# Start of a transformer block on one core: the order of the first loads and weight conversions, and identity matmuls ahead of the first rows

## The chip, the cores and the metric

The kernel runs on one core of a Trainium2 chip. The metric is the device time of one launch in microseconds. The runs shown of the kernel before gave 1534.84, 1535.05 and 1535.28 us, with a median of 1535.05 us.

## The reference

The input x is (2, 2048, 256) in fp32: 4096 rows (tokens) of 256 features. Cut to what matters, the reference computes

```
x = x + 0.5 * ffn(layernorm(x))
x = x + attention(layernorm(x))          # 16 heads of 16 features, softmax over 2048 keys
x = x + 0.5 * ffn(layernorm(x))

def ffn(x):                              # each weight is +1 or -1, from a boolean
    h = concatenate([x, -x], axis=-1)    # 512 features
    h = relu(s0 * (h @ where(k0, 1, -1))) * 2      # k0 (512, 1024)
    h = relu(s1 * (h @ where(k1, 1, -1))) * 2      # k1 (1024, 1024)
    return s2 * (h @ where(k2, 1, -1))             # k2 (1024, 256)
```

Only the start of the first ffn, on the first 512 rows, is touched by this change.

## The kernel before, in words

**Tiling.** The 4096 rows are cut into 8 blocks of 512 rows; a block is 4 tiles of 128 rows (`tpb = 4`). Block u goes through these steps, which a planner (`layers`, from line 146, and the list `side`, line 193) writes into one list `work`. Every engine then walks this list in order and issues its own share of each step.

- `norm`: VectorE takes the mean and variance of each row (`bn_stats`, `bn_aggr`) and forms 1/sqrt with a bit trick and three Newton rounds (`dve_norm`, line 947). The factor 64 times 2 times the sign of s0 (`scal[:, 12:13]`) is multiplied in there.
- `xn`: VectorE subtracts the mean and multiplies (`dve_xn`, line 992), four instructions, one for each tile.
- Turning features to partitions: for later blocks a DMA transpose does it. For block 0 alone TensorE does it (`turn_x`): for each of two feature halves m, four transposes of 128x128 against the identity `ident` into one PSUM bank. ScalarE then writes the fp16 rounded part of the bank to `xt[:, 0, m]`, and VectorE the fp16 rest to `xt[:, 1, m]`.
- `l1`: eight steps m, one for each 128 of the 1024 hidden features, four matmuls each (rounded part and rest, two halves of 128 features each). Since the second half of the concatenated input is -x, `w0` is the difference of two halves of k0 (`dve_w0`, line 600). ScalarE writes the rounded part `h0_hi` of each bank (L840), VectorE the rest `h0_lo` (L911).
- `l2`: eight steps of sixteen matmuls with `w1`: the eight rounded parts k = 0 to 7 first, then the eight rests. The first step waits for each `h0_hi[k]` and for each `w1[:, k]` as it comes to them.
- `l3` with `w2`, and for later steps the projections and the attention.

**Weights.** k0, k1 and k2 come as bytes. `w1` is made from k1 as fp16 in eight instructions of 128x1024: the four even k by ScalarE (`act_w1`, line 614), the four odd k by VectorE (`dve_w1`, line 608), all of them between `turn_x` and `l1` in the list. Two instructions of VectorE make `w0` columns 0 to 511 ahead of the turning and two make columns 512 to 1023 behind it. GpSimd makes the identity (L561, L564), then ten small instructions on the factors s0, s1, s2 (`pool_scalars`, line 580), then `w2` (L575) and scaled projection weights (L578).

**Loads.** They are issued ahead of all else, from two queues. ScalarE issues the three factors (4 bytes each, broadcast to 128 partitions) and k0 in two loads of 256 KB (`act_loads`, line 536). SyncE issues the four tiles of the first block (128 KB each), k1 in one load of 1 MB, block 1 (512 KB), k2, the projection weights and biases and block 2 (`sp_loads`, line 543).

**Order.** All engines are strictly in order on their lists. PSUM banks are handed out in a ring of seven in this part of the kernel; `l1` uses each at most once more, far behind its readers. For block 0 the list begins

```
side = norm_turn(0, 0) + [Step("w0", 0, 0)] + turns("turn_x", 0) + [Step("w0", 0, 1), Step("w1")]
side += [Step("l1", 0, m) for m in range(kh)]
```

TensorE's first wait is that all four tiles of `xn` are done (line 652). `norm` of block 1 stands in the list behind the second step of `l2` of block 0.

Of the kernel before, what the change touches and what calls it, by code (L numbers as in the profile page):

```python
# [13 lines left out]
ACT = mybir.ActivationFunctionType  # L14
ALU = mybir.AluOpType
AX = mybir.AxisListType

P = 128
# [5 lines left out]
class Step:  # L24
# [30 lines left out]
FILLS = {  # L55
    "turn_x": (4, (1, 1), (0, 2)),
    "l1": (4, (1, 1), (0, 2)),
# [30 lines left out]
def build(nc, x, wq, bq, wk, bk, wv, bv, wo_t, bo, k0, k1, k2, s0, s1, s2, out):  # L88
# [103 lines left out]

    side = norm_turn(0, 0) + [Step("w0", 0, 0)] + turns("turn_x", 0) + [Step("w0", 0, 1), Step("w1")]
    side += [Step("l1", 0, m) for m in range(kh)]
    for u in range(2 * blocks):
# [198 lines left out]
    with ExitStack() as ctx:  # L394
# [66 lines left out]
        def internal(name, shape, dt):  # L461
# [15 lines left out]
        k0_in = [sem(f"k0_in{k}") for k in range(kd)]  # L477
        scal_in, k1_in, k2_in, weights_in = (sem(n) for n in ("scal_in", "k1_in", "k2_in", "weights_in"))
        piece_out = [sem(f"piece_out{n}") for n in range(2 * kd)]
# [5 lines left out]
            sem(n) for n in ("consts", "scal_done", "table_seed", "table_ready"))  # L485
        w0_done, w1_act, w1_dve, w2_done, qk_scaled = (
            sem(n) for n in ("w0_done", "w1_act", "w1_dve", "w2_done", "qk_scaled"))

# [11 lines left out]
        CONSTS = 6  # L500
        IDENT = 3
        SCALARS = 10
        WEIGHTS_IN = 16 * 10
# [27 lines left out]
        def load_x(u):  # L531
            i = block_of(u)
            ts = slice(i * tpb, (i + 1) * tpb)
            sp.dma_start(x_sb[:, u % RING], (x_tiles if u < blocks else x1_tiles)[:, ts, :]).then_inc(x_in[u % RING], 16)

        def act_loads():
            for n, s in enumerate((s0, s1, s2)):
                act.dma_start(scal[:, n:n + 1], s.broadcast_to((P, 1))).then_inc(scal_in, 16)
            for k in range(kd):
                act.dma_start(k0_raw[:, k::kd, :], k0.rearrange("(h k p) n -> p k h n", p=P, k=kd)[:, k]  # L540
                              ).then_inc(k0_in[k], 16)

        def sp_loads():
            for t in range(tpb):
                sp.dma_start(x_sb[:, 0, t, :], x_tiles[:, t, :]).then_inc(x0_in[t], 16)
            sp.dma_start(k1_raw, k1.rearrange("(k p) n -> p k n", p=P)).then_inc(k1_in, 16)
            load_x(1)
            sp.dma_start(k2_raw, k2.rearrange("(k p) n -> p k n", p=P)).then_inc(k2_in, 16)
            for dst, src in ((wq_sb, wq), (wk_sb, wk), (wv_sb, wv), (wo_sb, wo_t)):
                sp.dma_start(dst[:], src.rearrange("(k p) n -> p k n", p=P)).then_inc(weights_in, 16)  # L550
            for dst, src in ((bq_sb, bq), (bk_sb, bk)):
                for k in range(kd):
                    sp.dma_start(dst[:, k:k + 1], src[k * hpt:(k + 1) * hpt].rearrange("h a e -> (h e) a")
                                 ).then_inc(weights_in, 16)
            sp.dma_start(bv_sb[:], bv.rearrange("h a e -> a (h e)").broadcast_to((P, dim))).then_inc(weights_in, 16)
            sp.dma_start(bo_sb[:], bo.rearrange("(a n) -> a n", a=1).broadcast_to((P, dim))).then_inc(weights_in, 16)
            for u in range(2, RING - 1):
                load_x(u)

        def pool_constants():  # L560
            pool.memset(ident[:], 0.0).then_inc(consts, 1)  # L561
            pool.memset(head_ones[:], 1.0).then_inc(consts, 1)
            pool.wait_ge(consts, 2)
            pool.affine_select(out=ident[:], in_=ident[:], compare_op=ALU.not_equal, fill=1.0, base=0,  # L564
                               pattern=[[-1, P]], channel_multiplier=1).then_inc(consts, 1)
            ho = head_ones[:].rearrange("p (h e) -> p h e", e=hd // 4)
            pool.affine_select(out=ho, in_=ho, compare_op=ALU.is_ge, fill=0.0, base=0,
                               pattern=[[-hd, hpt], [0, hd // 4]], channel_multiplier=1).then_inc(consts, 1)
            pool.wait_ge(consts, 4)
            pool.affine_select(out=ho, in_=ho, compare_op=ALU.is_ge, fill=0.0, base=hd - 1,  # L570
                               pattern=[[hd, hpt], [0, hd // 4]], channel_multiplier=-1).then_inc(consts, 1)
            pool.memset(v_sb[:, :, :, hd:va], 1.0).then_inc(consts, 1)
            pool_scalars()
            pool.wait_ge(k2_in, 16)
            pool.tensor_scalar(w2[:], k2_raw, 2.0, -1.0, ALU.mult, ALU.add).then_inc(w2_done, 1)  # L575
            pool.wait_ge(weights_in, WEIGHTS_IN)
            for w in (wq_sb, wk_sb, bq_sb, bk_sb):
                pool.tensor_scalar(w[:], w[:], QK_SCALE, 0.0, ALU.mult, ALU.add).then_inc(qk_scaled, 1)  # L578
# [21 lines left out]
        def dve_w0(m):  # L600

            cols = slice(m * hidden // 2, (m + 1) * hidden // 2)
            for k in range(kd):
                dve.wait_ge(k0_in[k], 16)
                dve.tensor_tensor(w0[:, k, cols], k0_raw[:, k, cols], k0_raw[:, kd + k, cols], ALU.subtract
                                  ).then_inc(w0_done, 1)

        def dve_w1():
            dve.wait_ge(k1_in, 16)
            for k in range(1, kh, 2):  # L610
                dve.tensor_scalar(w1[:, k, :], k1_raw[:, k, :], scal[:, 13:14], scal[:, 14:15], ALU.mult, ALU.add
                                  ).then_inc(w1_dve, 1)

        def act_w1():
            act.wait_ge(k1_in, 16)
            act.wait_ge(scal_done, SCALARS)
            for k in range(0, kh, 2):
                act.activation(w1[:, k, :], k1_raw[:, k, :], ACT.Identity, scale=scal[:, 13:14], bias=scal[:, 14:15]
                               ).then_inc(w1_act, 1)

        def pe_steps(steps):
            for s in steps:
# [12 lines left out]
                elif s.kind in FILLS and s.lo < s.hi:  # L637
                    pe_fill(s)

        def pe_fill(s):  # L640
            u, m, bank = s.u, s.m, s.bank
# [7 lines left out]
            for j in range(s.lo, s.hi):  # L649
                if s.kind == "turn_x":  # L650
                    if j == 0 and m == 0:
                        pe.wait_ge(ln_x, tpb)
                        pe.wait_ge(consts, IDENT)
                    mm = pe.transpose(psum[:, bank, j * P:(j + 1) * P], xn[:, 0, j, m * P:(m + 1) * P], ident[:])  # L654
                elif s.kind == "l1":
# [3 lines left out]
                    if u == 0 and m == 0 and half == 0:  # L659
                        wait_hi(pe, find["turn_x", u, k])  # L660
                        pe.wait_ge(w0_done, k + 1)
                    if u == 0 and m == kh // 2 and j < kd:
                        pe.wait_ge(w0_done, kd + k + 1)
                    if u == 0 and m == 0 and half == 1:
# [3 lines left out]
                elif s.kind == "l2":  # L668
                    half, k = divmod(j, kh)
                    if m == 0 and half == 0:  # L670
                        wait_hi(pe, find["l1", u, k])
                        if u == 0 and k % 2 == 0:
                            pe.wait_ge(w1_act, k // 2 + 1)
                        if u == 0 and k % 2 == 1:
                            pe.wait_ge(w1_dve, k // 2 + 1)
                    if m == 0 and half == 1:
# [148 lines left out]
        def act_steps(steps):  # L825
            for s in steps:
# [3 lines left out]
                elif s.kind == "w1":  # L830
                    act_w1()
                elif not s.on_act or s.kind not in FILLS or not s.last():
                    continue
                elif s.kind == "turn_x":
                    act.wait_ge(mm_done, s.mm)
                    act.activation(xt[:, 0, m, :], psum[:, bank, :], ACT.Copy).then_inc(act_done, 1)  # L836
                elif s.kind in ("l1", "l2"):
# [34 lines left out]
        def dve_steps(steps):  # L872
            for s in steps:
# [15 lines left out]
                elif s.kind == "w0":  # L889
                    dve_w0(m)  # L890
                elif s.kind == "w1":
                    dve_w1()
                elif s.kind not in FILLS or not s.last():
                    continue
                elif s.kind == "turn_x":
                    if s.on_act:
                        dve.wait_ge(act_done, s.act)
                    else:
                        dve.wait_ge(mm_done, s.mm)
                        dve.tensor_copy(xt[:, 0, m, :], psum[:, bank, :]).then_inc(dve_done, 1)  # L900
                        dve.wait_ge(dve_done, s.hi_dve)
                    dve.tensor_tensor(xt[:, 1, m, :], psum[:, bank, :], xt[:, 0, m, :], ALU.subtract).then_inc(dve_done, 1)
                elif s.kind in ("l1", "l2"):
# [43 lines left out]
        def dve_norm(s):  # L947
# [26 lines left out]
            for k in range(3):  # L974
                at_k = base + 2 * tpb + 4 + 3 * k
                dve.wait_ge(ln, at_k)
                dve.tensor_tensor(square_y, y, y, ALU.mult).then_inc(ln, 1)
                if k == 2 and n == 0:
                    dve.wait_ge(scal_done, SCALARS)
                if k == 2:  # L980

                    dve.tensor_scalar(root[:, 5, :], y, 1.0 if s.m == 1 else scal[:, 12:13], None, ALU.mult
                                      ).then_inc(ln, 1)
                    y, at_k = root[:, 5, :], at_k + 1
# [405 lines left out]
```

## Time and profile before

| what | value |
|---|---|
| median of 3 runs | 1535.05 us |
| profiled execution, its own time | 1535.96 us |
| span of the profiled execution | 1532.1 us |
| TensorE matmul busy | 1512.4 us, 99% |
| ScalarE busy | 1131.3 us, 74% |
| VectorE busy | 584.7 us, 38% |
| GpSimd busy | 59.9 us, 4% |

The profiled execution took 1535.96 us, of which the span from its first to its last instruction or transfer is 1532.1 us; 3.9 us lie around the span. Times in rows count from the start of the span. L with a number is a line of the kernel. PE is TensorE's matmul, PEld its weight load, DVE VectorE, ACT ScalarE, POOL GpSimd, SPq and ACTq the instructions by which SyncE and ScalarE issue a DMA.

### The profile page before, as it was taken

How to read it: one execution, taken by the hardware profiler on the slowest of the kernel's cores; microseconds unless marked ns; L12 is line 12 of the kernel's file. 1: busy time of each engine (PE TensorE's matmuls, PEld its weight loads, DVE VectorE, ACT ScalarE, POOL GpSimd, SP SyncE). 2: the span in 40 equal slices, each digit the busy share in tenths (PEclk: the TensorE clock that was granted, in tenths of full speed). 3: DMA queues.
4: the chain of work that ended last, by engine and by line, in shares of the span. 5: the costliest groups of instructions: out<-in, count | busy, mean ns of one | idle time of the engine just before them, and what ended most of it. 6: DMA issues, size and time to landing. Idle time of an engine off the chain costs nothing.

```text
span 1532.1 us, 31536 instructions
## 1 busy us (share of the span) xinstructions
PE 1512.4 (99%) x12441; PEld 600.0 (39%) x12441; DVE 584.7 (38%) x1329; ACT 1131.3 (74%) x1655; POOL 59.9 (4%) x65
## 2 busy tenths in 40 slices
PE   6999999999999999999999999999999999999999
PEld 3555455333333433433333333334334334333354
DVE  6556746511431252325332242232332323332372
ACT  3212221798898898888989888988988988998721
POOL 2010111000000010010010000000000000000000
PEclk9999999999999999999999999999999999999999
DMA  4231223212231331223212113112212211311110
GB/s 124 49 90 35 80 79 103 80 50 74 74 67 44 104 105 48 54 96 95 80 52 81 53 40 107 39 39 67 80 39 67 80 39 53 105 48 33 36 42 16
DMA packets 110515, 101.44 MB, mean 66 GB/s; under 512 B 56224, under 2 KB 95904, under 8 KB 110368
## 3 DMA queue, kind: packets, MB, share of 16 engines
q1 hardware_dynamic: 109392, 98.86, 22.5%
q8 instruction: 104, 1.70, 0.5%
q10 hardware_dynamic: 976, 0.53, 0.1%
q14 instruction: 43, 0.35, 0.1%
HBM read 61.87 MB, written 25.43 MB: 57 GB/s over the span
## 4 chain that ended last, share of the span: by engine, by line
PE 98%; DVE 1%; POOL 0%; DMA 0%; ACT 0%; issue 0%; SPq 0%; POOLq 0%; DVEq 0%
PE psum L811 31%; PE psum L775 29%; PE psum L795 16%; PE psum L678 12%; PE psum L690 3%; PE psum L666 3%; PE psum L697 2%; PE psum L711 1%; POOL square L1079 0%; DMA x_sb<-in_x 0%; PE psum L704 0%; DVE xn L1002 0%; PE psum L654 0%; ACT prob L867 0%; DVE h_lo L911 0%
## 5 line engine op out<-in xcount | busy, mean ns | idle before, releaser
L867 ACT ACTIVATE prob<-psum 128x512 f32<-128x512 f32 (+1 forms) x1440 | 1018.7, 783 | 122.5 <-PE psum L795 116.9
L811 PE MATMUL psum<-prob,v_sb 128*17 128x512 f32 x4096 | 490.2, 595 | 0.0
L795 PE MATMUL psum<-q_st,k_st 64*128 64x512 f16 x2048 | 350.1, 379 | 1.5 <-ACT prob L867 0.9
L840 ACT ACTIVATE h_hi<-psum 128x512 f16<-128x512 f32 x183 | 110.0, 604 | 217.2 <-PE psum L678 161.5
L909 DVE TENSOR_SCALAR h_hi<-psum 128x512 f16<-128x512 f32 x73 | 50.5, 692 | 431.2 <-PE psum L775 431.1
L911 DVE SCALAR_TENSOR_TENSOR h_lo<-psum,h_hi 128x512 f16<-128x512 f32 x256 | 168.5, 687 | 82.3 <-ACT h_hi L840 79.8
L811 PEld LDWEIGHTS psum<-prob,v_sb 128*17 128x17 f32 x4096 | 96.6, 96 | 261.3 <-issue 164.2
L795 PEld LDWEIGHTS psum<-q_st,k_st 64*128 64x128 f16 x2048 | 82.8, 94 | 279.5 <-ACT prob L867 209.3
L775 PE MATMUL psum<-h_hi,w 64*128 64x512 f16 x1184 | 151.9, 376 | 0.3 <-DVE h_lo L911 0.3
L775 PE MATMUL psum<-h_lo,w 64*128 64x512 f16 x1184 | 151.8, 376 | 0.0
L678 PE MATMUL psum<-h_hi,w 128*128 128x512 f16 x432 | 102.1, 379 | 0.0
L678 PE MATMUL psum<-h_lo,w 128*128 128x512 f16 x432 | 102.1, 379 | 0.0
L1046 DVE COPY o_sb<-psum 128x512 f32<-128x512 f32 x32 | 22.1, 691 | 168.8 <-PE psum L811 168.5
L775 PEld LDWEIGHTS psum<-h_hi,w 64*128 64x128 f16 x1184 | 58.0, 94 | 70.7 <-DVE h_lo L911 1.7
L775 PEld LDWEIGHTS psum<-h_lo,w 64*128 64x128 f16 x1184 | 57.7, 94 | 69.9
L775 PE MATMUL psum<-xn,w 64*128 64x512 f16 x576 | 74.3, 377 | 0.0
L916 DVE SCALAR_TENSOR_TENSOR x_sb<-psum,scal,x_sb 128x512 f32<-128x512 f32 x32 | 23.2, 749 | 108.3 <-PE psum L775 77.5
L678 PEld LDWEIGHTS psum<-h_lo,w 128*128 128x128 f16 x432 | 42.3, 98 | 51.0
L678 PEld LDWEIGHTS psum<-h_hi,w 128*128 128x128 f16 x432 | 42.1, 98 | 51.1 <-issue 0.7
L1079 POOL TENSOR_TENSOR square<-piece 128x512 bf16<-128x512 f16 x32 | 32.8, 1040 | 723.6 <-DVE piece L925 405.0
L1037 DVE RECIPROCAL den_t<-den_t 128x128 f32<-128x128 f32 x64 | 60.5, 945 | 0.0
L666 PE MATMUL psum<-xn,w 128*128 128x512 f16 x224 | 52.0, 388 | 0.2 <-ACT xn L836 0.2
(101 smaller groups left out, 870.8 us busy)
## 6 DMA issues: line engine op xcount, KB each, us to landing
k_st<-k_halves SPq DMA_DIRECT2D x64, 512.0 KB, 4.4
q_halves<-piece SPq DMA_DIRECT2D x32, 256.0 KB, 2.5
q_st<-q_halves SPq DMA_DIRECT2D x64, 128.0 KB, 4.9
x_rows<-x_sb SPq DMA_DIRECT2D x16, 256.0 KB, 2.2
k_halves<-piece SPq DMA_DIRECT2D x16, 256.0 KB, 2.9
att_rows<-o_sb SPq DMA_DIRECT2D x128, 32.0 KB
x_sb<-x_rows SPq DMA_DIRECT2D x8, 512.0 KB, 4.0
att_t<-att_rows SPq DMA_DIRECT2D x16, 256.0 KB
```

The source lines that it names most:

```text
L666: mm = pe.matmul(psum[:, bank, :], w0[:, k, m * P:(m + 1) * P], xt[:, half, k, :], start=(j == 0), stop=(j == s.n - 1))
L678: mm = pe.matmul(psum[:, bank, :], w1[:, k, m * P:(m + 1) * P], (h0_hi, h0_lo)[half][:, k, :], start=(j == 0), stop=(j == s.n - 1))
L690: mm = pe.matmul(psum[:, bank, t * dim:(t + 1) * dim], (h1_hi, h1_lo)[half][:, k, tile * P:(tile + 1) * P], w2[:, k, :], start=(jj == 0), ...
L775: mm = pe.matmul(to, w, a, start=(turned == 0 and j == 0), stop=(turned == 1 and j == length - 1))
L795: mm = pe.matmul(psum[:, score_bank[h + r], :], k_st[rows, slot, t * P:(t + 1) * P], q_st[rows, slot, :], start=True, stop=True)
L811: mm = pe.matmul(psum[32 * j:32 * j + va, O_BANK, :], v_sb[:, b * key_tiles + t, GROUP * g4 + j, :], prob[:, h % PROBS, :], start=(t == 0) ...
L840: act.activation(hi, psum[:, bank, :], ACT.Relu).then_inc(act_done, 1)
L867: act.activation(prob[:, to:to + count, :], psum[:, bank:bank + count, :], ACT.Exp, scale=score_scale / QK_SCALE ** 2).then_inc(exp_sem, 1)
L909: dve.tensor_scalar(hi[:, m, :], psum[:, bank, :], 0.0, None, ALU.max).then_inc(dve_done, 1)
L911: dve.scalar_tensor_tensor(lo[:, m, :], psum[:, bank, :], 0.0, hi[:, m, :], ALU.max, ALU.subtract).then_inc(dve_done, 1)
L1037: dve.reciprocal(den_t[:, half, cols], den_t[:, half, cols]).then_inc(den_inv, 1)
L1079: pool.tensor_tensor(square[:, m % 2, :], piece[:, m, 0, :], piece[:, m, 0, :], ALU.mult).then_inc(squared, 1)
```

## The change

The loads, the conversions and the list of the first block are put in another order, and TensorE gets matmuls that nobody reads.

- **Loads.** The fourth tile of rows goes from SyncE's queue to ScalarE's, behind the three factors and ahead of k0. SyncE issues tiles 0 to 2, waits for the fourth tile to land, then issues k1 in four loads of 256 KB with a semaphore each, then k2 and the projection weights; block 1 moves behind all of these.
- **w1.** VectorE's four instructions go to GpSimd, ahead of `w2` there. ScalarE's four are spread: one ahead of the `l1` steps 0, 2, 4 and 6 each.
- **w0.** Four steps of 256 columns in place of two of 512, the first ahead of `turn_x` 0, the second between `turn_x` 0 and 1, the others behind.
- **Factor.** The factor of s0 is no longer in block 0's norm; ScalarE and VectorE multiply it in when they read the turned bank.
- **TensorE.** 22 fp32 matmuls of the 128x128 identity with itself stand ahead of the first transpose. The transposes of m = 0 wait for one tile of `xn` each.

```diff
-    "turn_x": (4, (1, 1), (0, 2)),
+    "turn_x": (4, (1, 1), (1, 1)),
...
-    side = norm_turn(0, 0) + [Step("w0", 0, 0)] + turns("turn_x", 0) + [Step("w0", 0, 1), Step("w1")]
-    side += [Step("l1", 0, m) for m in range(kh)]
+    side = norm_turn(0, 0) + [Step("w0", 0, 0), Step("turn_x", 0, 0), Step("w0", 0, 1), Step("turn_x", 0, 1)]
+    side += [Step("w0", 0, 2), Step("w0", 0, 3)]
+    for m in range(kh):
+        side += [Step("w1", 0, m), Step("l1", 0, m)]
...
+        WARM_UP = 22
...
+        def load_x0(queue, t):
+            queue.dma_start(x_sb[:, 0, t, :], x_tiles[:, t, :]).then_inc(x0_in[t], 16)
+
         def act_loads():
             for n, s in enumerate((s0, s1, s2)):
                 act.dma_start(scal[:, n:n + 1], s.broadcast_to((P, 1))).then_inc(scal_in, 16)
+            load_x0(act, tpb - 1)
...
         def sp_loads():
-            for t in range(tpb):
-                sp.dma_start(x_sb[:, 0, t, :], x_tiles[:, t, :]).then_inc(x0_in[t], 16)
-            sp.dma_start(k1_raw, k1.rearrange("(k p) n -> p k n", p=P)).then_inc(k1_in, 16)
-            load_x(1)
+            for t in range(tpb - 1):
+                load_x0(sp, t)
+
+            sp.wait_ge(x0_in[tpb - 1], 16)
+            for n in range(kh // 2):
+                sp.dma_start(k1_raw[:, 2 * n:2 * n + 2, :], k1.rearrange("(k p) n -> p k n", p=P)[:, 2 * n:2 * n + 2, :]
+                             ).then_inc(k1_in[n], 16)
...
-            for u in range(2, RING - 1):
+            for u in range(1, RING - 1):
                 load_x(u)
...
             pool_scalars()
+            for k in W1_POOL:
+                pool.wait_ge(k1_in[k // 2], 16)
+                pool.tensor_scalar(w1[:, k, :], k1_raw[:, k, :], scal[:, 13:14], scal[:, 14:15], ALU.mult, ALU.add
+                                   ).then_inc(w1_pool, 1)
...
-            cols = slice(m * hidden // 2, (m + 1) * hidden // 2)
+
+            cols = slice(m * hidden // 4, (m + 1) * hidden // 4)
...
-        def dve_w1():
-            dve.wait_ge(k1_in, 16)
-            for k in range(1, kh, 2):
-                dve.tensor_scalar(w1[:, k, :], k1_raw[:, k, :], scal[:, 13:14], scal[:, 14:15], ALU.mult, ALU.add
-                                  ).then_inc(w1_dve, 1)
-
-        def act_w1():
-            act.wait_ge(k1_in, 16)
+
+        W1_ACT, W1_POOL = range(0, kh, 2), range(1, kh, 2)
+
+        def act_w1(k):
+            act.wait_ge(k1_in[k // 2], 16)
             act.wait_ge(scal_done, SCALARS)
-            for k in range(0, kh, 2):
-                act.activation(w1[:, k, :], k1_raw[:, k, :], ACT.Identity, scale=scal[:, 13:14], bias=scal[:, 14:15]
-                               ).then_inc(w1_act, 1)
+            act.activation(w1[:, k, :], k1_raw[:, k, :], ACT.Identity, scale=scal[:, 13:14], bias=scal[:, 14:15]
+                           ).then_inc(w1_act, 1)
...
+        def pe_warm_up(bank):
+
+            pe.wait_ge(consts, IDENT)
+            for n in range(WARM_UP):
+                pe.matmul(psum[:, bank, 0:P], ident[:], ident[:], start=True, stop=True)
...
                 if s.kind == "turn_x":
+                    if m == 0 and j == 0:
+                        pe_warm_up(bank)
+                    if m == 0:
+                        pe.wait_ge(ln_x, j + 1)
                     if j == 0 and m == 0:
-                        pe.wait_ge(ln_x, tpb)
                         pe.wait_ge(consts, IDENT)
...
-                    if u == 0 and m == kh // 2 and j < kd:
-                        pe.wait_ge(w0_done, kd + k + 1)
+                    if u == 0 and m in (2, 4, 6) and j < kd:
+                        pe.wait_ge(w0_done, kd * m // 2 + k + 1)
...
-                        if u == 0 and k % 2 == 0:
-                            pe.wait_ge(w1_act, k // 2 + 1)
-                        if u == 0 and k % 2 == 1:
-                            pe.wait_ge(w1_dve, k // 2 + 1)
+                        if u == 0 and k in W1_ACT:
+                            pe.wait_ge(w1_act, W1_ACT.index(k) + 1)
+                        if u == 0 and k in W1_POOL:
+                            pe.wait_ge(w1_pool, W1_POOL.index(k) + 1)
...
-                    act.activation(xt[:, 0, m, :], psum[:, bank, :], ACT.Copy).then_inc(act_done, 1)
+                    act.wait_ge(scal_done, SCALARS)
+                    act.activation(xt[:, 0, m, :], psum[:, bank, :], ACT.Copy, scale=scal[:, 12:13]).then_inc(act_done, 1)
...
-                    dve.tensor_tensor(xt[:, 1, m, :], psum[:, bank, :], xt[:, 0, m, :], ALU.subtract).then_inc(dve_done, 1)
+                    dve.wait_ge(scal_done, SCALARS)
+                    dve.wait_ge(act_done, s.act)
+                    dve.scalar_tensor_tensor(xt[:, 1, m, :], psum[:, bank, :], scal[:, 12:13], xt[:, 0, m, :],
+                                             ALU.mult, ALU.subtract).then_inc(dve_done, 1)
...
-                if k == 2 and n == 0:
-                    dve.wait_ge(scal_done, SCALARS)
                 if k == 2:
 
-                    dve.tensor_scalar(root[:, 5, :], y, 1.0 if s.m == 1 else scal[:, 12:13], None, ALU.mult
+                    if u and s.m != 1:
+                        dve.wait_ge(scal_done, SCALARS)
+                    dve.tensor_scalar(root[:, 5, :], y, 1.0 if s.m == 1 or u == 0 else scal[:, 12:13], None, ALU.mult
                                       ).then_inc(ln, 1)
```

## Rows read from the trace of the kernel before

**Rows 1.** The page, busy time and share of the span by engine.

```profile
PE 1512.4 (99%) x12441; PEld 600.0 (39%) x12441; DVE 584.7 (38%) x1329; ACT 1131.3 (74%) x1655; POOL 59.9 (4%) x65
```

**Rows 2.** Chain that ended last, by time: start us, us, what.

```profile
2.22 5.90 DMA x_sb<-in_x
...
8.14 0.44 DVE stats L960
...
11.61 1.39 DVE xn L1002 x4
...
13.05 1.98 PE psum L654 x8
...
15.05 0.61 ACT xn L836
...
15.71 8.39 PE psum L666 x31
...
100.42 6.87 PE psum L697 x16
```

**Rows 3.** Timeline, loads and rows: start us, us, what [idle before <-releaser].

```profile
0.79 1.37 ACTq L538 DMA_DIRECT2D scal<-in_s  x3
...
0.79 1.86 SPq L545 DMA_DIRECT2D x_sb<-in_x  x4
...
2.19 0.97 ACTq L540 DMA_DIRECT2D prob<-in_k  x2
...
4.07 0.85 DVE L960 BATCH_NORM_STATS2 stats<-x_sb 128x6 f32<-128x256 f32 x2 [2.57 <-DMA x_sb<-in_x]
...
6.71 0.25 POOL L582 TENSOR_SCALAR scal<-scal 128x3 f32<-128x3 f32 x1 [3.64 <-DMA scal<-in_s]
...
7.02 0.43 DVE L960 BATCH_NORM_STATS2 stats<-x_sb 128x6 f32<-128x256 f32 x1 [2.10 <-DMA x_sb<-in_x]
```

**Rows 4.** Windows: stretch, length, busy PE, PEld, DVE, ACT, POOL, clock, DMA share, GB/s.

```profile
4.00:5.00 1.00, 0.00 (x0) 0.00 (x0) 0.85 (x2) 0.68 (x2) 0.00 (x0) 1.00 0.18 57
6.00:7.00 1.00, 0.00 (x0) 0.00 (x0) 0.00 (x0) 0.00 (x0) 0.29 (x2) 1.00 1.07 375
```

**Rows 5.** Timeline, from the rows to the next block's norm.

```profile
12.91 1.29 DVE L605 TENSOR_TENSOR w<-prob 128x512 f16<-128x512 uint8 x2
...
14.20 0.60 ACT L836 ACTIVATE xn<-psum 128x512 f16<-128x512 f32 x1 [9.51 <-PE psum L654]
...
15.55 4.62 ACT L618 ACTIVATE w<-prob,scal 128x1024 f16<-128x1024 uint8 x4
15.68 0.69 DVE L902 TENSOR_TENSOR xn<-psum,xn 128x512 f16<-128x512 f32 x1 [0.16 <-ACT xn L836]
...
16.96 0.15 PEld L666 LDWEIGHTS psum<-xn,w 128*128 128x128 f16 x1 [0.28 <-issue]
...
18.67 4.93 PEld L666 LDWEIGHTS psum<-xn,w 128*128 128x128 f16 x23 [0.28 <-issue]
...
20.07 3.01 ACT L840 ACTIVATE h_hi<-psum 128x512 f16<-128x512 f32 x6
...
23.93 1.89 PE L678 MATMUL psum<-h_hi,w 128*128 128x512 f16 x8
...
32.27 1.39 DVE L960 BATCH_NORM_STATS2 stats<-x_sb 128x6 f32<-128x256 f32 x4
```

**Rows 6.** Timeline, GpSimd and identity.

```profile
1.29 0.29 POOL L564 TENSOR_SCALAR_AFFINE_SELECT ident<-ident 128x128 f32<-128x128 f32 x1 [0.23 <-POOL head_ones L562]
...
14.65 1.90 POOL L575 TENSOR_SCALAR w<-prob 128x2048 f16<-128x2048 uint8 x1 [5.54 <-DMA prob<-in_k]
...
19.39 0.95 POOL L578 TENSOR_SCALAR wq_sb<-wq_sb 128x512 f32<-128x512 f32 x1 [2.84 <-DMA bo_sb<-in_bo]
```

**Rows 7.** Windows at the end of the span.

```profile
1528.00:1530.00 2.00, 0.80 (x8) 0.47 (x5) 0.75 (x1) 0.00 (x0) 0.00 (x0) 1.00 0.02 4
1530.00:1531.00 1.00, 0.00 (x0) 0.00 (x0) 0.00 (x0) 0.00 (x0) 0.00 (x0) 0.97 0.46 163
```

More of the change, by code:

```diff
@@ L477, in build @@
         k0_in = [sem(f"k0_in{k}") for k in range(kd)]
-        scal_in, k1_in, k2_in, weights_in = (sem(n) for n in ("scal_in", "k1_in", "k2_in", "weights_in"))
+        k1_in = [sem(f"k1_in{n}") for n in range(kh // 2)]
+        scal_in, k2_in, weights_in = (sem(n) for n in ("scal_in", "k2_in", "weights_in"))
         piece_out = [sem(f"piece_out{n}") for n in range(2 * kd)]
@@ L485, in build @@
             sem(n) for n in ("consts", "scal_done", "table_seed", "table_ready"))
-        w0_done, w1_act, w1_dve, w2_done, qk_scaled = (
-            sem(n) for n in ("w0_done", "w1_act", "w1_dve", "w2_done", "qk_scaled"))
+        w0_done, w1_act, w1_pool, w2_done, qk_scaled = (
+            sem(n) for n in ("w0_done", "w1_act", "w1_pool", "w2_done", "qk_scaled"))
         mm_done, act_done, dve_done = sem("mm_done"), sem("act_done"), sem("dve_done")
@@ L830, in act_steps @@
                 elif s.kind == "w1":
-                    act_w1()
+                    if m in W1_ACT:
+                        act_w1(m)
                 elif not s.on_act or s.kind not in FILLS or not s.last():
@@ L890, in dve_steps @@
                     dve_w0(m)
-                elif s.kind == "w1":
-                    dve_w1()
                 elif s.kind not in FILLS or not s.last():
@@ L895, in dve_steps @@
                 elif s.kind == "turn_x":
[L896 to L901, printed above, removed]
-                    dve.tensor_tensor(xt[:, 1, m, :], psum[:, bank, :], xt[:, 0, m, :], ALU.subtract).then_inc(dve_done, 1)
+                    dve.wait_ge(scal_done, SCALARS)
+                    dve.wait_ge(act_done, s.act)
+                    dve.scalar_tensor_tensor(xt[:, 1, m, :], psum[:, bank, :], scal[:, 12:13], xt[:, 0, m, :],
+                                             ALU.mult, ALU.subtract).then_inc(dve_done, 1)
                 elif s.kind in ("l1", "l2"):
```

## The prediction

> **What bounds the kernel now.** I read the page first: TensorE is busy 99% of the span [rows 1], so from its first instruction it hardly ever waits, and what the other engines do later cannot give much. Next the chain that ended last [rows 2]. Before TensorE's work it has the load of the rows (landed at 8.12), statistics, normalization (11.61 to 13.00), eight transposes (13.05 to 15.03), ScalarE's read of the second bank (15.05 to 15.66), then `l1`. So the only time to be won is that before the dense part, and each microsecond by which `l2` of block 0 starts earlier should leave the end by one. Then the timeline of the first 24 us with the windows for the loads [rows 3 to 5], to see which wait ends last at each step. The end of the span I read only for the clock [rows 7].
>
> I work in two terms: how much earlier `xn` is complete, and how much shorter the way from there to `l2` gets (now 13.00 to 23.93, 10.93 us [rows 2, 5]).
>
> **Term 1, the rows.** Four tiles are issued in 0.79 to 2.65, 0.46 us each [rows 3]. The first has landed by 4.07, 3.3 us after its issue began. The third waits until 7.02 (issued at about 1.7, 5.3 us) and the fourth until 8.14 (issued at about 2.2, 5.9 us) [rows 3]. The transfers have a lull: 57 GB/s in 4 to 5 us, against 375 GB/s in 6 to 7 [rows 4]. Behind the lull the tiles share the engines with k0 (issued 2.19 to 3.16) and, as SyncE's next load, k1. The third factor, issued at about 1.7, also came only at 6.7 [rows 3], so the lull holds both queues.
> In the new order the fourth tile is issued by ScalarE behind three factors, at about 2.2 as now: the issue saves nothing. It no longer stands behind the third tile, it stands ahead of k0, and k1 and block 1 are away. Lower bound: the first tile's 3.3 us hold for it too, landing at 5.5. Upper bound: the lull stays, and it comes with the third tile, 7.2. It can hardly be later than now, since k0's halves behind it would have to be later too. I take 6.3, between the two: the lull falls in the time in which the big loads are being set up, and one of its three candidates (k1) is gone; k0 is not. The third and fourth tile then land together, and 0.2 us of statistics are no longer hidden. From the last landing to `xn`'s start the chain of VectorE stays (8.12 to 11.61; the factor as a constant instead of an operand is worth under 0.1, taken as nothing). The wait for the factors leaves this chain; they were done in time anyway (GpSimd started on them at 6.71 and the ten small ones take some 2.4 us). Gain: 8.12 - 6.3 - 0.2 = 1.6 us, bounds 0.7 and 2.6; `xn` is complete at 11.4.
> The Trainium skill ("DMA: Bandwidth & Descriptors", section "Issuing engines are not separate DMA queues") says that transfers from different issuing engines interleave on the same 16 engines and that another queue saves issue time only. By it the move to ScalarE's queue gives nothing, and the term is all due to k1's absence; the bounds above hold either way.
>
> **Term 2, from `xn` complete (X) to `l2`.** Step by step, with X = 13.00 before:
> - Transposes. Now 8 instructions at 0.22 each, the fourth read at 14.20 [rows 2, 5], X + 1.20. In the new order three of the first four run while `xn` is still being written; the fourth ends 0.05 + 0.43 after X. ScalarE's first read is X + 0.5 to X + 1.1; the second bank is ready at X + 1.0 to 1.45 and read by X + 1.6 to 2.05 (now X + 2.66).
> - VectorE. Two instructions of 128x512 take 1.29 [rows 5], so two of 256 columns about 0.65: `w0` to X + 0.65, rest of bank 0 X + 1.1 to 1.8 (0.69 [rows 5]), `w0` to X + 2.45, rest of bank 1 to X + 3.15. The fourth matmul of `l1` waits for this. Now the rest of bank 1 is ready at 16.37, X + 3.37, and the steps after the first go on at about 16.96. The gain here is only 0.25 us, because half of `w0` now stands between the two rests; the earlier transposes are mostly lost on it.
> - `l1`. Now the weight loads are 0.43 us apart from 16.96 on, and 0.214 from 18.67 on (4.93 / 23) [rows 5]. A stream of 512 columns in 0.43 us is the 1.2 GHz level, in 0.214 the 2.4 GHz one; TensorE had stood idle until 13.05. If the identity matmuls bring the higher level before the rows, the fourth matmul starts at X + 3.2 and 29 matmuls at 0.216 end the layer's issue at X + 9.45.
> - ScalarE is then the closest limit. Four `w1` at 1.13 apart (4.62 for four, 1.23 the last) and reads at 0.48 apart (3.01 for six, 0.60 the last) [rows 5]. Behind the read of step 1 (X + 4.45) come `w1`, two reads, `w1`, two reads, `w1`, two reads: 3 x 1.13 + 5 x 0.48 = 5.8, and the last read ends at X + 4.45 + 0.48 + 5.8 + 0.6 = X + 11.3. The eighth matmul of `l2` wants it at X + 9.45 + 7 x 0.216 = X + 10.95. A stall of 0.35 to 0.4 us; the rests by VectorE (0.69 each, eight matmuls later) follow in time.
> So `l2` starts, counted with its stall, at X + 9.9: 10.93 - 9.9 = 1.05 us gained. VectorE's four `w1` (now behind the turning) cost TensorE nothing before, so their going gives nothing.
>
> **Edits that I cost at nothing.** GpSimd's `w1`: 128x2048 bytes took 1.90, 128x512 of fp32 0.95 [rows 6]; one of 1024 is thus 0.95 to 1.9. With k1 issued from 6.4 the first quarter is there by about 10.5; four are done by 14.3 to 18.1, and `l2` wants the last at 22.3. `w2` and the projection scales queue behind them, and wait for 50 us and more of TensorE's work; if that cover were gone they would cost their own 4 to 8 us. k1, then k2 and the weights (4 MB with the rows, at 375 GB/s 11 us [rows 4]) are in by about 18 to 20; block 1 behind them is wanted by its statistics, now at 32.27 [rows 5], about 29.6 then. ScalarE's queue gets one issue more, 0.46, ahead of its table load, with nothing due before X. The identity matmuls: the trace has an ordinary fp32 matmul as two instructions (16 for the eight of a block's projections [rows 2]), so 44 instructions. At the transposes' 0.22 they take 9.7 us from 1.6 and end at 11.3; at half of that per instruction once the clock has risen, 8.6. The first tile of `xn` comes at about 10.4, the last at 11.4: at the upper bound the transposes wait for them by 1 us, of which VectorE's `w0` and rests hide most (under 0.5 shows).
>
> **Sum.** 1.6 + 1.05 = 2.65 us. The profiled execution's 1535.96 us (span 1532.1 and 3.9 around it) would become 1533.3. It lies 0.9 above the median of the runs; from the median, 1535.05 - 2.65 = 1532.4 us.
>
> **Rivals.**
> 1. *The lull goes with k1.* The tile lands at 5.5 as the first one did. Gain 2.6 + 1.05: 1531.4. For it: the first two tiles had 3.3 us. Against: k0 and the factors are still there.
> 2. *The lull stays.* Landing at 7.2; 0.7 + 1.05: 1533.3. For it: the third factor, in the queue where the fourth tile now goes, came at 6.7.
> 3. *The clock does not hold.* At the end of the span the last matmuls end at 1528.8 and the granted clock falls by about 1530.97 (0.97 of full over that microsecond, half after) [rows 7], some 2.1 us after them. Between the last identity matmul (8.6 to 11.3) and the dense `l1` (X + 3.2 = 14.6) stand only eight transposes and three matmuls. If TensorE is at 1.2 GHz there, 5 matmuls (if it rises as late after the first `l1` matmul, 14.85 to about 19, as now) to 10 (if it counts from 14.6) cost 0.214 more each: 1.05 to 2.1, less ScalarE's stall of 0.4, so about 1.2. Time 1533.6.
> The Trainium skill ("TensorE: Matmul & The Clock Gate", Part 4: PE-mode transpose) says that a transpose does not count as work for the clock. The trace of before fits, with eight transposes ending at 15.03 and the slow pace still there at 16.96; by that rule the stretch before `l1` is nearly idle and this rival gets its chance.
> 4. *Slower: GpSimd is late with w1.* `l2`'s first step waits for its quarters. It decides from (22.3 - 10.5) / 4 = 2.95 us for one instruction; the kernel is slower than before from 3.6. At 4.0 it stalls 4.2 us: 1536.6. For it: the two factor operands are not in any row of this size, and GpSimd took 0.95 for only 512 of fp32. Against: 1.90 for 2048 bytes, twice the columns of one quarter [rows 6].
>
> **How the numbers follow.** Forecast 0.45, rival 1 0.18, rival 2 0.14, rival 3 0.20, rival 4 0.03. The forecast's own range, from landings at 5.8 to 6.8, is 1531.9 to 1532.9. The whole range takes in rivals 1 to 3 with a part of their combinations: 1531.0 to 1534.2. A difference of 0.2% is 3.07 us, about what a measurement of this kernel tells from no change; below 1531.98 lie rival 1 and the low end of the forecast, 0.29. Above 1538.1 lies only the far end of rival 4, 0.01, and 0.70 is within.
>
> **What would show it.** Right: the last statistics of block 0 start near 6.3, `xn` ends near 11.4, TensorE's `l1` weight loads are 0.215 apart from its second step on, `l2` starts near 20.8 with a short wait for ScalarE at its eighth matmul, and everything behind is shifted by one amount. Wrong: spacing of 0.43 in `l1`; a last row later than 7.2; `l2` waiting for GpSimd; transposes waiting for identity matmuls; a gap at block 1's norm; or a span that shrinks by less than `l2`'s shift.

## The result, and the profile after

The changed kernel took 1540.03 us (median of 8 runs, 1538.74 to 1540.82), the kernel before 1535.23 (8 runs). The ratio is 1.0029, 95% interval 1.0020 to 1.0038: slower by 4.8 us where I had forecast 2.65 us faster, outside my range of 1531.0 to 1534.2.

Most of it lies in the span. The changed kernel's spans have a median of 1535.6 us and those of the kernel before 1531.2 (28 runs that stood beside the first experiments, 1530.1 to 1532.2; the profiled one of 1532.1 is at their long end). The rest lies outside the span: 4.44 us against 3.86. The two profiled executions, from which the lines here come, differ by less: spans of 1535.0 and 1532.1, 2.9 us, where the medians differ by 4.4.

The chain that ended last, after, by time (start us, us, what), against [rows 2]:

```profile
2.21 3.78 DMA x_sb<-in_x
...
6.02 0.44 DVE stats L978
...
9.07 1.05 DVE root L1004
...
10.36 1.12 DVE xn L1020
...
11.52 1.32 PE psum L675 x4
...
12.86 0.70 ACT xn L859
...
15.37 2.10 DVE w L621
17.47 0.67 DVE xn L919
...
18.19 8.74 PE psum L687 x29
```

The rows do come 2.1 us earlier (landed at 5.99 instead of 8.12). But three instructions in the chain last far longer than their like: one of the third Newton round, on 4 numbers for each partition, takes 1.05 us where its like took 0.17; the first `xn` takes 1.12 where the four together took 1.39 [rows 2]; and one `w0` instruction, which was not in the chain before, takes 2.10 where two of twice the size took 1.29 [rows 5]. TensorE's dense `l1` starts at 18.19, and at the slow pace.

The timeline of the same stretch, VectorE and GpSimd, after:

```profile
8.87 2.45 POOL L587 TENSOR_SCALAR w<-prob,scal 128x1024 f16<-128x1024 uint8 x2 [0.74 <-DMA prob<-in_k]
...
9.07 1.04 DVE L1004 TENSOR_TENSOR root<-root 128x4 f32<-128x4 f32 x1
...
10.36 2.07 DVE L1020 TENSOR_SCALAR xn<-x_sb,moment,rstd 128x256 f32<-128x256 f32 x4
...
11.85 3.33 POOL L587 TENSOR_SCALAR w<-prob,scal 128x1024 f16<-128x1024 uint8 x2 [0.53 <-DMA prob<-in_k]
...
13.67 0.75 DVE L919 SCALAR_TENSOR_TENSOR xn<-psum,scal,xn 128x512 f16<-128x512 f32 x1 [0.58 <-ACT xn L859]
...
14.34 3.13 DVE L621 TENSOR_TENSOR w<-prob 128x256 f16<-128x256 uint8 x2
...
15.15 2.05 POOL L590 TENSOR_SCALAR w<-prob 128x2048 f16<-128x2048 uint8 x1
...
17.39 0.74 DVE L919 SCALAR_TENSOR_TENSOR xn<-psum,scal,xn 128x512 f16<-128x512 f32 x1
```

Lay the two engines side by side. GpSimd's first `w1` runs from 8.87 to about 10.1, and VectorE's small instruction, which began at 9.07, ends at 10.11. The second `w1` runs to about 11.3, and the first `xn`, begun at 10.36, ends at 11.47. GpSimd's `w2` runs 15.15 to 17.20, and the `w0` instruction begun at 15.37 ends at 17.47. It goes the other way too: the third `w1`, begun at 11.85 beside `xn` and `w0`, takes about 2.15 where 1.19 is usual. The rests (L919), which read one operand from PSUM, take 0.75 while GpSimd works (13.67) and 0.74 when it does not (17.39). Nothing in the view calls this a wait: the blocked instruction simply has a long duration.

TensorE, after (timeline, then windows with the columns of [rows 4]):

```profile
1.63 7.17 PE L656 MATMUL psum<-ident 128*128 128x128 f32 x44 [1.63 <-POOL ident L575]
...
11.52 2.16 PE L675 MATMUL psum<-ident,xn 128*128 128x128 f32 x8 [2.72 <-DVE xn L1020]
...
18.19 8.10 PE L687 MATMUL psum<-xn,w 128*128 128x512 f16 x26 [2.70 <-DVE xn L919]
...
22.86 3.15 PEld L687 LDWEIGHTS psum<-xn,w 128*128 128x128 f16 x15 [0.28 <-issue]
```

```profile
12.50:13.00 0.50, 0.50 (x3) 0.50 (x4) 0.50 (x2) 0.14 (x1) 0.50 (x1) 0.67 1.12 335
...
13.00:13.50 0.50, 0.50 (x4) 0.27 (x2) 0.10 (x1) 0.50 (x1) 0.50 (x1) 0.50 1.11 344
...
22.50:23.00 0.50, 0.50 (x3) 0.21 (x2) 0.12 (x1) 0.34 (x1) 0.00 (x0) 0.59 0.00 0
```

The 22 identity matmuls are 44 instructions in the trace; they end at 8.80, and TensorE then idles 2.72 us. The clock fell from 2.4 to 1.2 GHz near 12.7 (0.67 and then 0.50 of full granted in those windows), in the transposes, and came back only near 22.9. The first 11 of the 29 dense `l1` matmuls are 0.43 us apart. `l2` starts at 26.77, against 23.93 before [rows 5]: 2.84 us later, which is the 2.9 of the profiled spans. The clock column has a blind spot: it reads 1.00 from the start until the first fall, also where the matmuls are 0.43 us apart, as before at 17 to 18.5 and in e3 below at 19 to 21. There the spacing of the matmuls tells the level and the column does not.

### The profile page after: what moved, and what is told of

Read it like the earlier page. It is cut to its first block, busy times and chain, and to the rows that moved or that the text cites. A ratio compares the mean times of both kernels' runs of the same rounds, so it can differ in the third digit from the quotient of the medians.

```text
span 1535.0 us, 31638 instructions
## 1 busy us (share of the span) xinstructions
PE 1521.2 (99%) x12485; PEld 606.4 (40%) x12485; DVE 586.3 (38%) x1329; ACT 1131.7 (74%) x1655; POOL 65.2 (4%) x69
## 4 chain that ended last, share of the span: by engine, by line
PE 97%; DVE 1%; POOL 0%; issue 0%; DMA 0%; ACT 0%; ACTq 0%; POOLq 0%; DVEq 0%
PE psum L832 31%; PE psum L796 29%; PE psum L816 16%; PE psum L699 12%; PE psum L711 3%; PE psum L687 3%; PE psum L718 2%; PE psum L732 1%; POOL square L1097 0%; PE psum L725 0%; DMA x_sb<-in_x 0%; DVE xn L1020 0%; DVE w L621 0%; ACT prob L890 0%; DVE root L1004 0%
```

## Experiments

Each time is a median, beside the runs of the kernel before on the same chip. Spans and the time outside are medians of all runs of a kernel.

| kernel | time, us | before beside it | ratio, 95% interval | span | outside |
|---|---|---|---|---|---|
| e1 GpSimd held back | 1534.56 | 1535.04 | 0.9999 (0.9989 to 1.0009) | 1530.05 | 4.47 |
| e2 only `w2` held back | 1537.54 | 1535.04 | 1.0016 (1.0007 to 1.0026) | 1533.1 | 4.41 |
| e3 no identity matmuls | 1539.32 | 1535.04 | 1.0027 (1.0016 to 1.0039) | 1534.7 | 4.48 |
| e4 before + new loads | 1534.41 | 1535.04 | 0.9996 (0.9986 to 1.0005) | 1529.95 | 4.43 |
| e5 e1 without identity matmuls | 1535.06 | 1535.35 | 0.9998 (0.9988 to 1.0008) | 1530.65 | 4.49 |
| e6 34 identity matmuls | 1539.07 | 1535.35 | 1.0026 (1.0016 to 1.0035) | 1534.6 | 4.5 |
| e7 e4 with one k1 load | 1533.50 | 1535.35 | 0.9987 (0.9978 to 0.9997) | 1529.6 | 3.96 |
| e8 e1 in a better order | 1533.57 | 1535.35 | 0.9988 (0.9979 to 0.9998) | 1529.15 | 4.44 |
| e9 e8 with one k1 load | 1532.43 | 1535.13 | 0.9981 (0.9972 to 0.9990) | 1528.5 | 4.00 |
| e10 e9 with filled gaps | 1531.97 | 1535.13 | 0.9978 (0.9969 to 0.9987) | 1527.6 | 4.23 |
| e11 e4, one semaphore | 1534.66 | 1535.13 | 0.9993 (0.9983 to 1.0002) | 1530.1 | 4.42 |

**e1, e2: is it GpSimd?** e1 adds to the changed kernel one wait ahead of GpSimd's `w1` (so `w2`, behind it, is late too); e2 has the same wait ahead of `w2` alone.

```diff
             pool_scalars()
+            pool.wait_ge(w0_done, 4 * kd)          # e1
             for k in W1_POOL:
...
+            pool.wait_ge(w0_done, 4 * kd)          # e2
             pool.wait_ge(k2_in, 16)
```

> The changed kernel, with GpSimd's four w1 and its w2 held back until VectorE has finished all eight w0 instructions. Theory A (VectorE and GpSimd block each other on SBUF access): the norm's small instruction is back at 0.16 us, xn at 1.4, each w0 at 0.41; xn complete near 11.4, the dense part of l1 starts near 14.7 instead of 18.2. TensorE's clock is down by then, so l1 runs half of its way at 0.43 us and l2 starts near 23.3, 3.6 earlier; time about 1536. Theory B (the slow instructions come from the transfers that write SBUF in that stretch, or from a late k0): nothing of this moves, l2 at 26.9, time 1540.

> The changed kernel with only GpSimd's w2 held back behind VectorE's w0; its w1 stay early. Theory A: the norm and xn stay slow (xn complete at 12.4), only the w0 instruction of 2.10 us falls to 0.4, so everything from the second rest on comes 1.7 us earlier: dense l1 at 16.5, time about 1538.3. Theory B: no change, 1540.

Timeline of e1:

```profile
11.15 0.75 DVE L622 TENSOR_TENSOR w<-prob 128x256 f16<-128x256 uint8 x2
...
13.14 0.75 DVE L622 TENSOR_TENSOR w<-prob 128x256 f16<-128x256 uint8 x2
...
14.61 6.43 PE L688 MATMUL psum<-xn,w 128*128 128x512 f16 x29 [0.94 <-DVE xn L920]
...
15.99 4.72 POOL L588 TENSOR_SCALAR w<-prob,scal 128x1024 f16<-128x1024 uint8 x4 [7.82 <-DVE w L622]
...
20.88 2.36 PE L700 MATMUL psum<-h_hi,w 128*128 128x512 f16 x8
...
23.07 1.89 PE L700 MATMUL psum<-h_lo,w 128*128 128x512 f16 x8
```

With the same transfers and the same instructions, all VectorE durations are back (the longest `w0` is 0.42) and GpSimd's four take 1.19 each. `xn` is complete at 11.24, dense `l1` starts at 14.61 instead of 18.19. That is theory A, the two engines blocking each other; theory B, the transfers or a late k0, is out. It gives 5.5 us of 1540.03, more than the 4 I had expected, since the clock also stayed up in this profiled execution (29 matmuls in 6.43). From the two profiled executions, `l2` starts 5.89 us earlier than in the changed kernel: 3.58 because dense `l1` starts earlier, 2.31 because its 29 matmuls run at the full pace; 0.37 of it is lost again in a longer wait for ScalarE, and the spans differ by 5.5.

The clock did not stay up in every run of e1. Five of its ten runs have a mean granted clock of 1.000 and spans of 1529.2 to 1529.7, the other five 0.998 or 0.999 and 1530.4 to 1531.9; the changed kernel has 0.996 or 0.997 in all eight.

e2 gives 2.5 us, 0.8 more than the one instruction: of 5.5 us, `w2` is 2.5 and `w1` the other 3.0.

**e3, e5, e6, the identity matmuls.** `WARM_UP` is 0 in e3 (on the changed kernel) and e5 (on e1), and 34 in e6 (on the changed kernel).

> The changed kernel without its 22 identity matmuls. If their clock is lost before the dense part of l1 begins (theory A): l1 is at the 1.2 GHz pace as with them, and the time is the same within 0.5 us, 1540. If they still help: slower by 1 to 2 us. If they cost something by themselves (instructions, a late first transpose): faster by some tenths.

> GpSimd's conversions held back as in e1, and no identity matmuls. With them the clock stayed at 2.4 GHz from 6.9 us on and l2 started at 20.9. Theory: the matmuls are worth the half-pace stretch of l1, less the part that ScalarE would hold back anyway: clock up near 17 to 18.5, l2 near 22, span 0.5 to 1.2 us longer than e1's 1530.0, time about 1535.4. Rival: ScalarE hides all of it, same as e1 within 0.3 us.

> The changed kernel with 34 identity matmuls in place of 22; nothing is held back. They should end near 11.4 instead of 8.8, so TensorE is not idle before the transposes. If the idle stretch of 2.7 us before the transposes lost the clock, it is now still up in l1 and the span is up to 2 us shorter than the changed kernel's 1535.6. If VectorE's stall by GpSimd (no matmul from 15.4 to 18.2) loses it again: same as the changed kernel.

In the changed kernel they gain nothing: without them it took 0.7 us less, with ratios that overlap (1.0027 and 1.0029). On e1 they seem worth 0.5 us, but e1's spans (1529.2 to 1531.9) and e5's (1529.3 to 1531.9) overlap fully: not a shown gain. In the two profiled executions `l2` starts at 20.88 with them and 22.82 without; half of e1's runs lost the clock, and that hides it. e6's matmuls end at 10.9, its clock fell near 14.8 and came back near 21.6; its 1.0 us less is not clear of noise either (ratio 1.0026). In e6 TensorE still idles 1.04 us ahead of the transposes and 0.72 within them, and the clock is down before the long idle stretch (16.3 to 18.3), as in the changed kernel (12.7, ahead of 15.5 to 18.2). So it is not that stretch that loses the clock; which of the gaps ahead of it does is not shown.

**e4, the loads alone.** The kernel before with the changed `act_loads` and `sp_loads`; `w1`, `w0` and TensorE's list as before.

> The kernel before with only the new loads (fourth tile on ScalarE's queue, k1 in four parts behind the rows, block 1 behind the weights). The last tile lands near 6.0 instead of 8.1; w1 by VectorE and ScalarE as before, so the norm is undisturbed: xn complete at 10.9, l2 at 21.9, time 2.1 us under the kernel before, 1533.1. Rival: k1 comes too late for w1 and l1 waits for VectorE, 1535.

Its timeline:

```profile
9.90 1.38 DVE L1010 TENSOR_SCALAR xn<-x_sb,moment,rstd 128x256 f32<-128x256 f32 x4
...
13.85 1.90 POOL L583 TENSOR_SCALAR w<-prob 128x2048 f16<-128x2048 uint8 x1 [5.69 <-DMA prob<-in_k]
...
14.58 2.31 DVE L613 TENSOR_TENSOR w<-prob 128x512 f16<-128x512 uint8 x2
...
21.61 1.89 PE L686 MATMUL psum<-h_hi,w 128*128 128x512 f16 x8
```

`l2` starts 2.3 us earlier, the profiled span is 2.2 shorter than that of before (medians: 1.25), but the time only 0.6. The block by GpSimd is there too (two `w0` in 2.31 instead of 1.29, beside `w2`), but TensorE is busy without a gap from 14.0 on, so it costs nothing. Of the median's 1.25, 0.57 went outside the span, 3.86 to 4.43 us; all kernels with four k1 loads have 4.4 to 4.5 there.

**e7, e11: what costs outside the span.**

```diff
-            for n in range(kh // 2):
-                sp.dma_start(k1_raw[:, 2 * n:2 * n + 2, :], ...).then_inc(k1_in[n], 16)
+            sp.dma_start(k1_raw, ...).then_inc(k1_in[0], 16)                              # e7
+            for n in range(kh // 2): sp.dma_start(..., ...).then_inc(k1_in[0], 16)        # e11
```

> e4 (the kernel before with the new loads) with k1 in one load and one semaphore in place of four. e4's span was 2.3 us shorter than the kernel before, its time only 0.6: outside the span it had 4.43 us against 3.86. Theory: the three more loads and semaphores cost that; outside back at 3.9, time 1533.9. Rival: it comes from the fourth tile on ScalarE's queue or from the hold of k1; outside stays at 4.4.

> e4 with its four k1 loads on one semaphore (its readers wait for all four). If the semaphores cost the 0.5 us outside the span, it falls to 3.9; if the three more loads do, it stays at 4.4. The span is e4's, 1530.0, or a few tenths more.

One load instead of four brings 0.47 us back; four loads on one semaphore bring nothing. It is the three more loads, then, not their semaphores and not the hold or ScalarE's queue. How three loads make time outside the recorded span I can't say. What they do within it is not clear of the spread: e4's spans are 1529.1 to 1530.8, e7's 1529.0 to 1530.2.

**e8, e9, e10: a version that beats both.** e8 is e1 with both rests ahead of the second `w0` step, and one `w1` taken from ScalarE; GpSimd starts behind it. e9 loads k1 in one piece. e10 adds identity matmuls in TensorE's gaps.

```diff
-    side = norm_turn(0, 0) + [Step("w0", 0, 0), Step("turn_x", 0, 0), Step("w0", 0, 1), Step("turn_x", 0, 1)]
-    side += [Step("w0", 0, 2), Step("w0", 0, 3)]
+    side = norm_turn(0, 0) + [Step("w0", 0, 0), Step("turn_x", 0, 0), Step("turn_x", 0, 1)]
+    side += [Step("w0", 0, 1), Step("w0", 0, 2), Step("w0", 0, 3), Step("w1v", 0, 6)]      # w1[:, 6] by VectorE
...
-        W1_ACT, W1_POOL = range(0, kh, 2), range(1, kh, 2)
+        W1_ACT, W1_POOL = (0, 2, 4), range(1, kh, 2)
...
-            pool.wait_ge(w0_done, 4 * kd)
+            pool.wait_ge(w1_dve, 1)
...
-        WARM_UP = 22
+        WARM_UP = 26                       # e10, and 2, 1 and 2 more: ahead of l1's first, second and fourth matmul
```

> e1 with VectorE's order mended: both rests of the turned banks ahead of the second w0 step, one of ScalarE's four w1 (k = 6) by VectorE behind its w0, and GpSimd starting behind that. The dense part of l1 should start near 14.0 instead of 14.6, ScalarE should no longer hold l2's eighth matmul: l2 near 20.2, its second half 1.1 us earlier than e1's, span about 1529.0, time 1533.4. Rival: GpSimd, now starting 0.9 us later, is late with its last w1: no gain over e1.

> e8 with k1 in one load. e7 brought the time outside the span back from 4.4 to 3.96 us, and it should here: span as e8's, 1529.1, time 1533.0, 2.3 us under the kernel before. Rival: k1 as a whole lands after 12.4 us, when ScalarE wants its first part, and some of the gain is lost in the span.

> e9 with 26 instead of 22 identity matmuls ahead of the rows and five more in TensorE's gaps ahead of l1's first four matmuls. Theory: e8's clock fell at 12.3 and rose at 15.7, in its gaps; fuller, it stays at 2.4 GHz through l1, but VectorE and ScalarE are the limit by then, so the span is 0 to 0.7 us shorter than e9's. Rival: the added matmuls delay the transposes and the first matmuls of l1 and the span is up to 0.5 us longer.

Timeline of e10, TensorE:

```profile
6.83 3.18 PE L655 MATMUL psum<-ident 128*128 128x128 f32 x27
9.96 1.73 PE L678 MATMUL psum<-ident,xn 128*128 128x128 f32 x8
...
13.58 6.42 PE L692 MATMUL psum<-xn,w 128*128 128x512 f16 x29
19.84 1.89 PE L708 MATMUL psum<-h_hi,w 128*128 128x512 f16 x8
21.57 1.89 PE L708 MATMUL psum<-h_lo,w 128*128 128x512 f16 x8
```

TensorE has no gap any more from 1.6 us on, `l1` takes 0.216 a matmul and `l2` runs without a stall from 19.84, 4.1 us earlier than in the kernel before. All its spans lie in 1527.6 to 1527.9, where e9's lie in 1527.5 to 1529.0 and the kernel before's in 1530.4 to 1532.3. e9's four runs with a mean granted clock of 1.000 lie in 1527.5 to 1527.9 too, and its seven with less in 1528.3 to 1529.0; e10 has 1.000 in all eleven. So what the added matmuls give is that the clock is held every time. Outside the span e10 has 0.23 us more. Its time is 1531.97, 3.2 us under the kernel before; the 0.5 us between it and e9 are within their intervals. e8 reached 1533.57 as expected, e9 a little under its 1533.0. In e8's profiled execution the windows have the clock down from about 12.0 to 15.3, not 12.3 to 15.7 as e10's expectation says.

## Why the prediction was wrong

- **The rows: right.** Landing at 5.99 (forecast 6.3, bounds 5.5 and 7.2). In e1, where nothing disturbs the norm, `xn` is complete at 11.24 against 11.4. The part that called ScalarE's queue worth nothing was not tested by itself.
- **The way from there to `l2`: right where nothing disturbs it.** e1 has dense `l1` at X + 3.37 (3.2), `l2` at X + 9.64 (9.45), and a stall of ScalarE in its eight first matmuls of 0.46 (0.35 to 0.4): 23.07 - 20.88 = 2.19 where eight take 1.73. e1's profiled span is 2.6 us under that of before, as in my sum. The medians are not: e1's span is 1.15 us under, and its time outside 0.6 over. Two things are in this. I read 2.65 us from an execution 0.9 longer than the median and took them off the median; why the kernel before spreads is not shown. And half of e1's runs lost the clock: the five that held it have a median span of 1529.4, 1.8 under.
- **The step that failed: "Edits that I cost at nothing", GpSimd's `w1`.** I asked only when GpSimd would be done, never what its instructions do to VectorE's while both run. With `w2` behind them they cost 0.88 us in the norm (9.07 to 10.11 for 0.16), 0.69 in `xn` (2.07 for 1.38), 0.7 and 1.7 in the second `w0` step (3.13 for two of 0.41 that overlap to 0.75). In place of the nothing that I put for this term stand 5.5 us, gained when GpSimd is held back (e1): 3.58 for the late dense `l1` and 2.31 for its slow pace, less 0.37. This alone turns the sign. Of it 2.5 come by `w2` (e2), which ran at nearly the same time before (14.65 against 15.15). There it met the `w0` behind both rests, and met it again in e4 at no cost to TensorE; in the changed kernel a `w0` stands between the rests, and the rest that `l1` waits for is behind it. The new order without `w1` on GpSimd was not run. With the 0.6 outside the span and the 1.5 of the point above it makes up the 7.6 us between 1532.4 and 1540.03. The trace of before had a sign of it, in the two `w0` instructions behind the rest, beside the end of GpSimd's `w2` (14.65 to 16.55 [rows 6]):

```profile
16.29 1.40 DVE L605 TENSOR_TENSOR w<-prob 128x512 f16<-128x512 uint8 x2
```

They took 1.40 against 1.29 [rows 5], one of them 0.80 against 0.68. I read neither.

The Trainium skill ("SBUF — State Buffer", section "Who interferes with whom") has the rule: VectorE and GpSimd share one pair of ports, and whoever starts first holds it for its whole instruction, if VectorE runs in a two-port mode, or has two inputs in SBUF while GpSimd reads SBUF. The traces agree: two-input instructions wait to GpSimd's end (10.11, 17.47), GpSimd waits for `xn` and `w0`, and the rests, with one operand in PSUM, wait for nothing (0.75 and 0.74). The first `xn`, with one tensor from SBUF, waits too (1.10 us for 0.40); by the page that would be a two-port mode, which no view here shows.

- **Rival 3, the clock: right in kind.** It fell near 12.7, ahead of the dense `l1`; I gave this 0.20 and 1.2 us, and it cost 2.31 in `l1` against e1. The step above made it worse: TensorE's gap ahead of the transposes is 2.72 us where e1 has 1.17, and the changed kernel lost the clock in all eight runs, e1 in five of ten. e6, with that gap cut to 1.04, still lost it.
- **Rival 4 had the right engine and the wrong victim.** GpSimd was never late for `l2`: its `w1` instructions took 1.19 undisturbed, far under the 2.95 from which that rival decides.
- **Time outside the span: taken as fixed.** It grew by 0.57 us, and one k1 load in place of four takes 0.47 of it back (e7, e11).

## What to carry to other kernels

Work moved to GpSimd is not free because GpSimd is idle: put it where VectorE reads PSUM, and look at each VectorE instruction that takes its tensors from SBUF and runs beside it, those with two of them first. Durations five times those of their like were waits here, though no view lists them as such. Matmuls that only keep the clock up are worth something only if the clock lasts to the dense matmuls: with a gap of 2.7 us behind them it never did here, with 1.2 us in five runs of ten (e1), with all gaps filled in eleven of eleven (e10); these kernels differ in more than the gap. And a gain in the span is only a gain if the time around it is looked at too.

## What the runs showed that I had not expected

- A VectorE instruction on 4 numbers for each partition took 1.04 us beside a GpSimd conversion of 128x1024, and one of 128x256 took 2.10 beside one of 128x2048.
- Four loads of 256 KB instead of one of 1 MB cost 0.47 us outside the span (4.43 against 3.96).
- Identity matmuls in fp32, 128x128: 44 instructions ended at 8.80 from 1.63; the last 16 of e9's took 1.95 us in all, at 2.4 GHz about 0.11 from one to the next, as against the 0.22 of the transposes before, at 1.2 GHz.
- The spread of the span goes with the clock where the column can show it: e1's and e9's runs fall into those with 1.000 (spreads of 0.5 and 0.4 us) and those below it, 0.8 to 2.7 us longer than the shortest of the same kernel.
